# Last stage of a five-part single-core kernel: attention products without zero halves, one sine operation, and the local mask as bf16 products of TensorE

## What is computed

```python
qkv = x @ Wqkv
q, k, v = split(qkv, 3, -1)                 # 16 heads of 64
q = l2norm(q) * qs
k = l2norm(k) * ksc
q = q * cos * scale + rotate_half(q) * sin * scale
k = k * cos * inv + rotate_half(k) * sin * inv
# local attention: each window of 32 queries sees the 32 keys before it and its own 32
mask = (it < jb) | (it > jb + w) | (jb == -1)
sim = einsum('bhwie,bhwje->bhwij', bq, bk2) * QK_SCALE
sim = where(mask, -finfo.max, sim)
attn = softmax(sim, -1)
out = einsum('bhwij,bhwje->bhwie', attn, bv2)
return out @ Wo
```

## Time and profile before

| | us |
|---|---|
| median of 3 runs | 4824.44 |
| lowest and highest run | 4803.81, 4836.79 |
| span of the profiled execution, first to last instruction | 4799.2 |
| last stage, first to last projection of TensorE | 1556 to 4708 |
| TensorE busy, whole span | 4554.0 |
| GpSimd, VectorE, ScalarE busy, whole span | 3692.6, 3761.7, 3501.1 |

### The profile page before, as it was taken

The page is one execution under the profiler, slowest core; times in us unless marked ns, Lnnn a source line. Parts: engine busy times, 40 slices in busy tenths (PEclk is TensorE's granted clock), DMA queues, the critical chain, the costliest instruction groups (busy, mean ns, idle before and its releaser), DMA issues.

```text
span 4799.2 us, 114895 instructions
## 1 busy us (share of the span) xinstructions
PE 4554.0 (95%) x44512; PEld 3128.6 (65%) x44512; DVE 3761.7 (78%) x5226; ACT 3501.1 (73%) x6738; POOL 3692.6 (77%) x2336
## 2 busy tenths in 40 slices
PE   7998999987887799999999999999999999999997
PEld 5666768874443466666666666666666666666665
DVE  6776556658999688888888888888888888888885
ACT  3454756557775688888888888888888888888885
POOL 2222334438998999999999999999999999999993
PEclk9898999998999999999999999999999999999998
DMA  2000000004332222232222322232322322322222
GB/s 79 1 2 1 2 1 1 1 1 168 150 142 106 55 63 63 56 85 70 54 67 65 75 68 55 68 75 61 68 64 67 76 53 66 80 64 63 62 56 52
DMA packets 164292, 289.06 MB, mean 60 GB/s; under 512 B 44063, under 2 KB 61351, under 8 KB 159655
## 3 DMA queue, kind: packets, MB, share of 16 engines
q1 hardware_dynamic: 162310, 281.46, 22.3%
q10 hardware_dynamic: 1440, 0.24, 0.0%
HBM read 90.22 MB, written 2.62 MB: 19 GB/s over the span
## 4 chain that ended last, share of the span: by engine, by line
PE 59%; ACT 3%; issue 2%; DVE 1%; POOL 1%; ACTq 0%; DVEq 0%; POOLq 0%
PE ps L2559 18%; PE ps L2614 8%; PE ps L2588 8%; PE ps L2572 7%; PE ps L2627 7%; PE ps L2601 3%; PE ps L2669 3%; PE ps L2660 3%; PE ps L2653 3%; ACT L3f_pT L2820 2%; PE ps L2634 1%; PE ps L2640 1%; ACT L3f_kT L2803 1%; POOL L3f_t L3155 0%; POOL L3f_raw L3172 0%
## 5 line engine op out<-in xcount | busy, mean ns | idle before, releaser
L3155 POOL TENSOR_TENSOR L3f_t<-L3f_raw,L3f_rot 128x512 f32<-128x512 f32 x768 | 1007.7, 1334 | 268.3 <-DVE L3f_raw L2971 268.3
L2559 PE MATMUL ps<-L3f_wqkv,all_z 128*128 128x512 f32 x2304 | 1133.7, 601 | 12.8 <-DVE L3f_raw L2971 11.7
L3172 POOL TENSOR_TENSOR L3f_raw<-L3f_raw,L3f_t 128x1024 f32<-128x1024 f32 x384 | 961.4, 2504 | 3.8
L3164 POOL TENSOR_TENSOR L3f_raw<-L3f_raw,L3f_rot 128x1024 f32<-128x1024 f32 x384 | 953.8, 2484 | 3.8
L2971 DVE TENSOR_TENSOR L3f_raw<-ps,L3f_ri 128x512 f32<-128x512 f32 x768 | 495.6, 682 | 231.9 <-ACT L3f_ri L2778 230.2
L2954 DVE TENSOR_REDUCE L3f_ss<-L3f_sqr 128x8 f32<-128x512 f32 x768 | 507.8, 681 | 163.2 <-ACT L3f_sqr L2768 160.8
L2572 PEld LDWEIGHTS ps<-all_ident,L3f_raw 128*128 128x128 f32 x3072 | 358.7, 141 | 320.7 <-issue 282.8
L2559 PEld LDWEIGHTS ps<-L3f_wqkv,all_z 128*128 128x128 f32 x2304 | 385.2, 191 | 221.0 <-issue 151.5
L2572 PE MATMUL ps<-all_ident,L3f_raw 128*128 128x128 f32 x3072 | 472.3, 276 | 49.1 <-ACT L3f_kT L2803 27.1
L2820 ACT ACTIVATE L3f_pT<-ps 64x512 f32<-64x512 f32 x768 | 453.2, 590 | 83.9 <-PE ps L2601 75.9
L2768 ACT ACTIVATE L3f_sqr<-ps 128x512 f32<-128x512 f32 x768 | 449.9, 599 | 76.5 <-PE ps L2559 71.7
(11 more groups left out here) (333 smaller groups left out, 8702.0 us busy)
## 6 DMA issues: line engine op xcount, KB each, us to landing
L3f_vw<-L3f_v SPq DMA_DIRECT2D x1344, 128.0 KB, 2.4
L3a_Bs<-L3a_rows SPq DMA_DIRECT2D x16, 2048.0 KB, 7.1
L3a_Cs<-L3a_rows SPq DMA_DIRECT2D x16, 2048.0 KB, 11.6
L3f_vw<-L3f_v SPq DMA_DIRECT2D x192, 64.0 KB, 2.1
L3f_wqkv<-in_L_ffn_Wqkv SPq DMA_DIRECT2D x24, 256.0 KB, 2.9
L3f_wqkv<-in_L_ffn_Wqkv SPq DMA_DIRECT2D x6, 512.0 KB, 3.6
L3f_wo<-in_L_ffn_Wo SPq DMA_DIRECT2D x48, 64.0 KB, 2.3
out<-all_x SPq DMA_DIRECT2D x8, 256.0 KB, 3.6
```

What stands on the lines that cost most here:

```text
L2559: p.matmul(PS[:, j % 3, :], Z[:, u % NSEQ, t * P:t * P + P], w, start=True, stop=True).then_inc(proj.sem)
L3155: op = g.tensor_tensor(t[:, :, to], r[:, :, fr], w[:, 1, to].unsqueeze(1).broadcast_to((P, H, WIN)), ALU.mult)
L3164: g.tensor_tensor(r, r, w[:, 0, :].unsqueeze(1).broadcast_to((P, H, HD)), ALU.mult).then_inc(cosined.sem)
L3172: g.tensor_tensor(r, r, t, ALU.add).then_inc(rotated.sem)
```

## The change

Scores: `qz` becomes `qT`, the turned q without zeros, and each head's product is one of its own, with 64 rows and 32 weight columns. The four windows take the four blocks of 32 partitions and the two heads of a pair the banks 6 and 7: 64 products a tile. Ahead of them two bf16 products of the identity and the mask over 512 columns fill banks 6 and 7, and VectorE's addition `hidden` goes. Values: `pT` is the plain turned probabilities, each head's product has 64 rows, 64 weight columns and 32 moving columns, and goes to bank 4 or 5 by head: 64 products a tile. The copies `turned` for q and `spread` become one operation each. The layouts of `sm`, `oT` and the mask follow. The sine becomes one operation, reading the two halves in reverse order by a negative step. The zeroing of `qz` and `pT` goes.

```diff
-        lmaskb = self.sb("lmaskb", [P, TILES, 2, KEYS], BF16)
+        lmaskb = self.sb("lmaskb", [P, TILES, KEYS], BF16)
...
-        qz = self.sb("qz", [P, TILES, PAIRS, NW, 2, WIN])
+        qT = self.sb("qT", [P, TILES, PAIRS, P])
-        sm = self.sb("sm", [P, TILES, H, KEYS])
+        sm = self.sb("sm", [P, TILES, PAIRS, 2, KEYS])
-        pT = self.sb("pT", [P, TILES, 2 * PAIRS, 2, 2, WIN])
-        oT = self.sb("oT", [P, TILES, PAIRS // 2, NW, 2, WIN])
+        pT = self.sb("pT", [P, TILES, PAIRS, P])
+        oT = self.sb("oT", [P, TILES, 2, PAIRS // 2, P])
...
+                for h in range(2):
+                    p.matmul(PS[:, 6 + h, :], identb[:, :], lmaskb[:, t, :].unsqueeze(1).broadcast_to((P, PAIRS, KEYS)), start=True, stop=False, skip_group_check=True)
                 for a in range(PAIRS):
                     for w in range(NW):
-                        r = slice(w % 2 * HD, w % 2 * HD + HD)
-                        mm = p.matmul(PS[r, 6 + w // 2, a * KEYS:(a + 1) * KEYS], qz[:, t, a, w, :, :].rearrange("p h q -> p (h q)"),
-                                      kT[:, a, t * P + w * WIN:t * P + w * WIN + KEYS], start=True, stop=True)
+                        for h, (r, _) in enumerate(halves):
+                            mm = p.matmul(PS[w * WIN:(w + 1) * WIN, 6 + h, a * KEYS:(a + 1) * KEYS], qT[r, t, a, w * WIN:(w + 1) * WIN],
+                                          kT[r, a, t * P + w * WIN:t * P + w * WIN + KEYS], start=False, stop=True, skip_group_check=True)
                 mm.then_inc(scored.sem)
...
                 for c in range(PAIRS // 2):
                     for w in range(NW):
-                        for r in range(2):
-                            a = 2 * c + r
-                            mm = p.matmul(PS[r * HD:(r + 1) * HD, 4 + c // 2, (c % 2) * 256 + w * HD:(c % 2) * 256 + (w + 1) * HD],
-                                          vw[:, u % 2, t * NW + w, a * HD:(a + 1) * HD],
-                                          pT[:, t, w // 2 * PAIRS + a, w % 2, :, :].rearrange("p h q -> p (h q)"), start=True, stop=True)
+                        for to, n in halves:
+                            a = 2 * c + n
+                            for h, (r, _) in enumerate(halves):
+                                mm = p.matmul(PS[to, 4 + h, c * P + w * WIN:c * P + (w + 1) * WIN], vw[r, u % 2, t * NW + w, a * HD:(a + 1) * HD],
+                                              pT[r, t, a, w * WIN:(w + 1) * WIN], start=True, stop=True)
...
-                    for half in range(2):
-                        r = slice(half * HD, half * HD + HD)
-                        op = a.activation(qz[r, t, 4 * g:4 * g + 4, :, half, :], src[r, :, :].rearrange("p c (w q) -> p c w q", q=WIN), ACT.Copy)
+                    op = a.activation(qT[:, t, 4 * g:4 * g + 4, :], src, ACT.Copy)
...
-                for r in range(2):
-                    for half in range(2):
-                        op = a.activation(pT[half * HD:(half + 1) * HD, t, r:2 * PAIRS:2, :, half, :],
-                                          PS[r * HD:(r + 1) * HD, 4:6, :].rearrange("p b (n w h q) -> p (b n) w h q", w=2, h=2, q=WIN)[:, :, :, half, :], ACT.Copy)
-                op.then_inc(pT_in.sem)
+                a.activation(pT[:, t, :, :].rearrange("p a q -> p (a q)"), PS[:, 4:6, :].rearrange("p b n -> p (b n)"), ACT.Copy).then_inc(pT_in.sem)
...
-            def hidden(u, t):
...
-                v.tensor_tensor(x, x, lmaskb[:, t, :, :].unsqueeze(2).broadcast_to((P, 2, PAIRS, KEYS)), ALU.add).then_inc(s_mask.sem)
...
-                v.tensor_tensor(sm[:, t, :, :], sc(), mx[:, t, :].unsqueeze(2).broadcast_to((P, H, KEYS)), ALU.subtract).then_inc(s_sub.sem)
+                v.tensor_tensor(sm[:, t, :, :, :].rearrange("p a h k -> p h a k"), sc().rearrange("p (h a) k -> p h a k", h=2),
+                                mx[:, t, :].rearrange("p (h a) -> p h a", h=2).unsqueeze(3).broadcast_to((P, 2, PAIRS, KEYS)), ALU.subtract).then_inc(s_sub.sem)
...
-                for half in range(2):
-                    to, fr = slice(half * WIN, (half + 1) * WIN), slice((1 - half) * WIN, (2 - half) * WIN)
-                    op = g.tensor_tensor(t[:, :, to], r[:, :, fr], w[:, 1, to].unsqueeze(1).broadcast_to((P, H, WIN)), ALU.mult)
-                op.then_inc(sined.sem)
+                g.tensor_tensor(t.rearrange("p h (b e) -> p h b e", b=2), r.rearrange("p h (b e) -> p h b e", b=2)[:, :, ::-1, :],
+                                w[:, 1, :].rearrange("p (b e) -> p b e", b=2).unsqueeze(1).broadcast_to((P, H, 2, HD // 2)), ALU.mult).then_inc(sined.sem)
...
-        g.memset(qz[:, :, :, :, :, :], 0.0)
-        v.memset(pT[:, :, :, :, :, :], 0.0)
```

More of the change, by code:

```diff
@@ L2347, in L3f @@
     def L3f(self):
-        nc, d, PS, Z, ident = self.nc, self.d, self.PS, self.Z, self.ident
+        nc, d, PS, Z, ident, identb = self.nc, self.d, self.PS, self.Z, self.ident, self.identb
         DEPTH, H, HD, WIN = 6, 16, 64, 32
@@ L2450, in L3f @@
         load_scales(0, nc.sync)
-        lmask = rot[:, 1, 0, :, :].rearrange("p (t b) k -> p t b k", b=2)
+        lmask = rot[:, 1, 0, 0:TILES, :]
         nc.sync.dma_start(lmask, d["c_local"]).then_inc(got_m.sem, 16)
@@ L2465, in L3f @@
         nc.vector.wait_ge(*got_m.at(0, 15))
-        nc.vector.tensor_copy(lmaskb[:, :, :, :], lmask).then_inc(made.sem)
+        nc.vector.tensor_copy(lmaskb[:, :, :], lmask).then_inc(made.sem)
         yield
@@ L2600, in turn_p @@
                 for n in range(PAIRS):
[L2601 removed]
+                    mm = p.transpose(PS[:, 4 + n // 4, (n % 4) * P:(n % 4 + 1) * P], sm[:, t, n, :, :].rearrange("p h k -> p (h k)"), ident[:, :])
                 mm.then_inc(p_turned.sem)
@@ L2626, in project_out @@
                     for h in range(2):
-                        mm = p.matmul(PS[:, 4, 0:SEQ], wo[:, c, h, :], oT[:, :, c, :, h, :], start=(c + h == 0), stop=(c + h == PAIRS // 2))
+                        mm = p.matmul(PS[:, 4, 0:SEQ], wo[:, c, h, :], oT[:, :, h, c, :], start=(c + h == 0), stop=(c + h == PAIRS // 2))
                 mm.then_inc(w_mm.sem)
@@ L2809, in exponent @@
                 a.wait_ge(*s_sub.at(u, t))
-                a.activation(sm[:, t, :, :], sm[:, t, :, :], ACT.Exp, scale=QK_SCALE).then_inc(s_exp.sem)
+                x = sm[:, t, :, :, :].rearrange("p a h k -> p (a h k)")
+                a.activation(x, x, ACT.Exp, scale=QK_SCALE).then_inc(s_exp.sem)
             def spread(u, t):
@@ L2975, in sc, with top @@
                 return PS[:, 6:8, :].rearrange("p b (a k) -> p (b a) k", k=KEYS)
-            def hidden(u, t):
+            def top(u, t):
                 if not 0 <= u < N:
@@ L2980, in hidden @@
                 v.wait_ge(*scored.at(u, t))
-                x = PS[:, 6:8, :].rearrange("p b (a k) -> p b a k", k=KEYS)
-                v.tensor_tensor(x, x, lmaskb[:, t, :, :].unsqueeze(2).broadcast_to((P, 2, PAIRS, KEYS)), ALU.add).then_inc(s_mask.sem)
-            def top(u, t):
-                if not 0 <= u < N:
-                    return
-                v.wait_ge(*s_mask.at(u, t))
                 v.tensor_reduce(mx[:, t, :], sc(), AX.X, ALU.max).then_inc(s_max.sem)
@@ L3001, in total @@
                 v.wait_ge(*s_exp.at(u, t))
-                v.tensor_reduce(sl[:, t, :], sm[:, t, :, :], AX.X, ALU.add).then_inc(s_sum.sem)
+                v.tensor_reduce(sl[:, t, :], sm[:, t, :, :, :].rearrange("p a h k -> p (a h) k"), AX.X, ALU.add).then_inc(s_sum.sem)
             def share(u, t):
@@ L3013, in scale @@
                 v.wait_ge(*s_inv.at(u, t))
-                v.tensor_tensor(sm[:, t, :, :], sm[:, t, :, :], sl[:, t, :].unsqueeze(2).broadcast_to((P, H, KEYS)), ALU.mult).then_inc(s_mul.sem)
+                x = sm[:, t, :, :, :].rearrange("p a h k -> p (a h) k")
+                v.tensor_tensor(x, x, sl[:, t, :].unsqueeze(2).broadcast_to((P, H, KEYS)), ALU.mult).then_inc(s_mul.sem)
             def residual(u):
@@ L3083, in dve @@
             norm(2 * i + 3, "k0b")
-            hidden(2 * i + 2, 0)
             top(2 * i + 2, 0)
@@ L3096, in dve @@
             norm(2 * i + 3, "k1b")
-            hidden(2 * i + 2, 1)
             top(2 * i + 2, 1)
@@ L3117, in dve @@
             scale(2 * i + 2, 1)
-            hidden(2 * i + 3, 0)
             top(2 * i + 3, 0)
@@ L3125, in dve @@
             norm(2 * i + 4, "q1b")
-            hidden(2 * i + 3, 1)
             top(2 * i + 3, 1)
@@ L3197, in pool @@
             add(2 * i + 4, "k0")
-        g, v = nc.gpsimd, nc.vector
-        g.memset(vw[:, :, 0, :], 0.0).then_inc(zeroed.sem)
-        g.memset(kT[:, :, 0:WIN], 0.0)
-        g.memset(qz[:, :, :, :, :, :], 0.0)
-        v.memset(pT[:, :, :, :, :, :], 0.0)
+        nc.gpsimd.memset(vw[:, :, 0, :], 0.0).then_inc(zeroed.sem)
+        nc.gpsimd.memset(kT[:, :, 0:WIN], 0.0)
         for k in range(-1, N + 4):
@@ L3230, in constants @@
     first = seen & ((p[:, None] >= 32) | (k >= 32))
-    local = np.where(np.stack([first, seen], 1), 0.0, NEG).astype(np.float32)
```

(3 more changed lines are left out.)

6 lines of the change are left out of this document (3 added, 3 removed).

## The result

The kernel became slower: 4911.2 us (median, 4899.7 to 4923.1) against 4818.9 us of the kernel before, run beside it; the ratio is 1.020, 95% interval 1.016 to 1.024. The profiled execution's span rose from 4799.2 to 4920.2 us, by 121 us. The forecast was 4750 us and the range ended at 4890, so the sign and the range were both wrong.

A forecast was written before the change was run, and what follows sets the result against it. TensorE was taken to bound the kernel. Scores -119, values 0, mask +83 and +12, stall -48, start -2 sum to -74 us: span 4799 to 4725, plus 25.2 to the median, 4750 us; range 4650 to 4890.

The forecast's parts named there:

- How fast can they be handed over?: Divided scores on TensorE: MATMULs start about 7 ns apart in a burst of four; 1.25 us taken for a tile's 128.
- The scores' term: Scores block on TensorE: 128 smaller MATMULs take 1.25 us instead of 1.87, 0.62 us less a tile, x 192 = -119 us.
- The prediction's own sign of being wrong: Prediction is wrong if scores take over 1.7 us, values move by 0.3, or the chain runs over GpSimd.
- slower rival with a fixed price of a start: Scores and values: each MATMUL start costs 27 ns however small, 3.46 us per 128; about 5480 us, chance 0.05.
- Four at once in the scores: Only four score MATMULs overlap, so scores stay at 1.87 us with the mask on top; 4869 us, chance 0.18.
- values above 2.3 us: Deciding point for the rival that row halves do not overlap once columns are divided; values 3.74 us, 5228 us, chance 0.09.
- The values, 0 us: Values block on TensorE: 128 MATMULs in four places, paced by 64-column weight loads, still take 1.87 us; no change.
- The mask, +83 and +12: Two bf16 mask products before each tile's scores, 0.43 us x 192 = +83; extra switching of divided state, 0.25 x 48 = +12.
- ScalarE and the stall, -48: Shorter ScalarE copies end TensorE's 0.70 us wait for kT, x 48 = -34 us; smaller waits give 14 us back.
- VectorE, GpSimd, start: VectorE's dropped mask addition and GpSimd's single sine are hidden under TensorE; dropping pT's zeroing at the stage's start gives -2 us.

## Why the prediction was wrong, by its own steps

- **How fast can they be handed over?** This step failed. It took a burst of four for a pace that lasts 256 instructions, noted that such a run "is twice as dense and more than anything here", and priced that only inside the scores' block (1.25 us for 0.94), with nothing for instructions that come late. The array keeps up: an undisturbed block takes 1.41 us to the next block's start, its eight MATMULs at a time start some 7 ns apart, the next eight 56 ns later at best and 80 ns in the mean. What does not keep up is the stream of instructions, 3.2 us a packet at the closest. The scores' term, -119 us, measured -0.589 us a tile at best, -113, before the holes.
- **The holes** were no term at all. From means less least, 0.642 + 0.198 + 0.016 us a tile, x 192 = +164 us; holes of over 0.3 us are 142 of it, the rest shorter ones and time at the lower clock. That exceeds the whole forecast gain of 74. The prediction's own sign of being wrong, scores above 1.7 us, came true: 2.06 in the mean.
- **No rival was this one.** The slower rival with a fixed price of a start (27 ns each) says 3.46 us for each of the two blocks; the values' 128 starts run in 2.00 us. It was the nearest in spirit: something counted by instruction and not by columns. Four at once in the scores gives 4869, closer in time than the forecast, but for a reason that the blocks of 1.41 us deny. The "values above 2.3 us" point was not reached either (2.20, and 2.00 undisturbed).
- **The values, 0 us:** right for the block (1.998 for 1.990), wrong for its effect on the blocks beside it; two kernels that differ in the values and the copies around them alone are 111 us apart.
- **The mask, +83 and +12:** right in size (0.525 us with the switch, against 0.53). What it costs in the time is less: taking it off TensorE gives back 19 us where both parts are divided (4911 to 4892) and 32 where the scores alone are (4800 to 4768), since the scores get later without it (2.36 us in the mean for 2.06, and 1.92 for 1.66).
- **ScalarE and the stall, -48:** right, a little large: L2572 waits 1.1 us in the stretch where it waited 27.2, the chain has no pT, and the account above gives -34 to all but scores, mask and values, with +12 of `turn_p` in it, which the smaller waits do not explain. ScalarE is at 1717 / 79 = 21.7 us a sequence (forecast 22), VectorE at 25.0 (25).
- **VectorE, GpSimd, start:** right. The sine is 2478 ns (forecast 2.5 us) and worth nothing alone. Of the start's 2 us nothing can be told apart.

With supply left out the steps give -45 us by measured blocks, against -74 forecast. The row that would have warned was on the page before: 357 packets, of which 234 in 2700 us are one in 11.5 us, and 192 x 128 more instructions in each of two blocks that stand back to back raise the peak, not only the mean.

The prediction's two places on the Trainium skill: the page "TensorE: Matmul & The Clock Gate" has a least distance of about 25 ns between starts ("Wait — 56ns, not 53.3ns?"), and the runs disagree, 128 starts in 1.41 us being 11 ns each; its Part 3, that row and column blocks compose, agrees with the scores' twice as many MATMULs over the same columns in 1.41 us for 2.00. A page of the Trainium skill that the prediction did not use, "Runtime: NRT & Kernel Launch", section "Instruction fetch mechanics", says that instructions come in blocks of 16 KiB, 256 each, by a DMA queue of the engine's own; the counts above agree, 256 and 255 a packet. It also says that fetching is hidden, since instructions are issued more slowly than they come; here 87 holes say the opposite.

## What to carry to other kernels

Splitting a product into smaller ones that run side by side can save array time, and it multiplies instructions: besides the array's time, count TensorE's instructions (loads too, and two MATMULs per fp32 product) over every stretch of a few microseconds, and compare with what this kernel could be fed, 256 in 3.2 us at the closest. Idle time marked "issue" inside a block of equal products is the sign, and the proof is that every such hole begins at the same place in a count by 256. Where it shows, fewer and larger instructions, or light work between dense blocks, help; but the light work must come from a place where nothing else waits for it.

## What was not expected of the hardware

- TensorE's instructions come at most once per 3.2 us in packets of 256, and the work resumes up to 1.6 us after a packet's end. A mean of one packet in 7.0 us (2700 / 384) is far below that and still not safe: 68 of 158 blocks were late.
- Every hole begins where a packet's 256 instructions end: 87 of 87 here, and all 451 in the ten other kernels with divided blocks.
- The holes also lower TensorE's clock: eight falls to 1.2 GHz in 2700 us, each within 2 us after a hole of 1.5 to 2.2 us, and none in the kernel before. Two kernels compared by their medians can differ by this alone, as the one with half the keys does.
- Eight MATMULs of 64 rows by 32 columns run side by side with their fp32 weight loads, at 56 ns per eight at best and 80 in the mean: 128 take 1.27 us from the first start to the last and 1.41 to the next block's.
